# In the last tile of each sample, the first gate and value product is issued ahead of the next sample's projection

## The reference

```
x = x + tanh(g_xattn) * LN(rs * (softmax(clip(q k^T / sqrt(32))) v @ Wo^T + bo)) * gamma + beta   # q from LN(x), k and v from 64 context tokens, 16 heads
x = x + tanh(g_ffn) * bit_linear(silu(bit_linear(LN(x), gate_w)) * bit_linear(LN(x), val_w), out_w)
bit_linear(x, w): each token of x is scaled by 127 / max|x| and rounded to integers, w is rounded to -1, 0, 1 times its mean |w|
```

## Time and profile before

| | |
|---|---|
| time, median of 3 runs | 772.79 us (772.76 to 773.64) |
| the profiled execution's own time | 772.76 us |
| its span in the profile | 771.0 us |
| busy: TensorE, VectorE, ScalarE, GpSimd | 92%, 81%, 69%, 41% of the span |
| one pass of the loop body | about 80.2 us |

### The profile page before, as it was taken

One profiled execution on the slowest core, in us unless ns is written; L12 is line 12 of the kernel. 1 busy time (PEld: TensorE's weight loads), 2 busy tenths in 40 slices (PEclk: granted clock), 3 DMA queues, 4 the chain that ended last, 5 costly groups with the idle time before them and its releaser, 6 DMA issues.

```text
span 771.0 us, 13495 instructions
## 1 busy us (share of the span) xinstructions
PE 706.6 (92%) x4204; PEld 341.1 (44%) x4253; DVE 622.7 (81%) x1290; ACT 535.4 (69%) x701; POOL 316.9 (41%) x482
## 2 busy tenths in 40 slices
PE   4989755878999999999999999999999999999997
PEld 3434434433544454445444444444444544454443
DVE  6868797697778987798779877987798778778885
ACT  4575778977657956786678856795588657856554
POOL 4310315223554356344643454346444553354440
PEclk9999886989999999999999999999999999999999
DMA  9864426121453354435443354326433542244312
GB/s 324 254 232 124 116 83 212 42 39 45 113 130 67 83 111 105 106 82 109 95 116 82 80 124 90 85 63 129 106 79 81 115 96 62 55 93 86 83 42 69
DMA packets 177386, 81.07 MB, mean 105 GB/s; under 512 B 156595, under 2 KB 156851, under 8 KB 176710
## 3 DMA queue, kind: packets, MB, share of 16 engines
q1 hardware_dynamic: 177350, 80.62, 42.7%
HBM read 38.75 MB, written 10.51 MB: 64 GB/s over the span
## 4 chain that ended last, share of the span: by engine, by line
PE 37%; DVE 33%; issue 10%; ACT 6%; DMA 5%; another core or an unknown queue 5%; POOL 2%; SPq 1%; DVEq 0%; POOLq 0%; ACTq 0%
PE psum L1739 12%; PE psum L1705 11%; PE psum L1730 5%; DVE psum L1227 3%; DVE hmax L1240 2%; DMA arena<-x_both 2%; PE psum L1709 2%; DVE arena L1235 2%; PE psum L1932 2%; ACT arena L921 2%; DVE xmax L1312 2%; DVE stats L1300 2%; DVE arena L1346 2%; DVE stats L1266 2%
## 5 line engine op out<-in xcount | busy, mean ns | idle before, releaser
L1705 PE MATMUL psum<-ternary,xqT 128*128 128x512 f16 x1024 | 259.6, 382 | 3.2 <-DVE xqT L1257 1.1
L1705 PEld LDWEIGHTS psum<-ternary,xqT 128*128 128x128 f16 x1024 | 98.3, 98 | 120.3 <-DVE arena L1232 2.8
L665 POOL TENSOR_TENSOR rstd<-var_e,minus_half 128x1 f32<-128x1 f32 x64 | 39.8, 623 | 211.1 <-DVE var_e L1304 111.1
L1730 PE MATMUL psum<-ternary,arena 128*128 128x512 f16 x496 | 121.7, 379 | 1.5 <-DMA arena<-arena 1.5
L855 ACT ACTIVATE arena<-psum,dequant 128x512 f32<-128x512 f32 x128 | 87.1, 681 | 49.7 <-PE psum L1709 47.4
L1739 PE MATMUL psum<-wo_hi,arena 128*128 128x512 f16 x256 | 82.6, 384 | 0.3
L1240 DVE TENSOR_REDUCE hmax<-arena 128x1 f32<-128x1024 f32 x64 | 77.6, 1213 | 0.8
L1739 PE MATMUL psum<-arena,wq_hi 128*128 128x512 f16 x256 | 76.1, 379 | 1.7 <-DMA arena<-x_both 1.1
L863 ACT ACTIVATE arena<-arena,round_c,hscale 128x1024 f32<-128x1024 f32 x62 | 73.5, 1235 | 1.9 <-DVE hscale L1252 1.9
L895 ACT ACTIVATE arena<-arena,round_c 128x1024 f16<-128x1024 f32 x62 | 70.8, 1142 | 0.3
L1730 PEld LDWEIGHTS psum<-ternary,arena 128*128 128x128 f16 x496 | 46.2, 98 | 54.8 <-issue 3.8
(11 more groups left out here) (213 smaller groups left out, 1302.1 us busy)
## 6 DMA issues: line engine op xcount, KB each, us to landing
arena<-in_x SPq DMA_DIRECT2D x64, 256.0 KB, 2.8
out<-arena SPq DMA_DIRECT2D x31, 256.0 KB, 2.4
arena<-in_L_ffn_gate_w SPq DMA_DIRECT2D x4, 1024.0 KB, 12.9
arena<-in_L_ffn_out_w SPq DMA_DIRECT2D x3, 1024.0 KB, 4.9
ternary<-in_L_ffn_val_w SPq DMA_DIRECT2D x2, 1024.0 KB, 11.9
kcur<-k_scratch SPq DMA_DIRECT2D x56, 32.0 KB, 2.2
arena<-arena SPq DMA_TRANSPOSE x90, 3.1
ternary<-in_ctx SPq DMA_DIRECT2D x1, 1024.0 KB, 5.4
```

The source lines that it names most:

```text
L1705: ins = M.matmul(ps[:], xqT[:, t % 2, k, :], w[:, k, cols], start=(k == 0), stop=(k == KC - 1 and not biased))
L1730: ins = M.matmul(psO[:], hidT[t % 2][:, k, :], wo2[:, k, :], start=(k == 0), stop=(k == FC - 1))
```

## The change

In tile 3 of every sample, TensorE issues `gate_val(3, 0)` ahead of `project` (before: behind it). VectorE does `hidden(3, 0)` ahead of `statistics` (before: behind it), and `new_x` and `x_shift` behind `hidden(3, 1)` (before: behind `hidden(3, 0)`). No instruction is added or removed; ScalarE, GpSimd and the DMA queues keep their order. For b = 7 the attention part is off, so `project`, `statistics` and `new_x` are not there in tile 3 and the order stays as it was.

```diff
# VectorE, body
                     down = prev if t == 0 else ffn
+                    if ffn and t == NT - 1:
+                        hidden(t, 0)
                     if out_w_now and t == 0:
                         x_stats(c, t)
                     else:
                         statistics(update, pre, *nxt, t)
                     for n in range(NCH):
...
-                        if ffn:
+                        if ffn and (t < NT - 1 or n):
                             hidden(t, n)
...
-                        if n == 0:
+                        if n == (1 if ffn and t == NT - 1 else 0):
                             if update:
                                 new_x(*nxt)
                             if pre:
                                 x_shift(c, t)
# TensorE, body
                     attend = att and t == 2
+                    if ffn and t == NT - 1:
+                        gate_val(t, 0)
                     if update:
...
                             project(*nxt)
                     for i in range(NCH):
-                        if ffn:
+                        if ffn and (t < NT - 1 or i):
                             gate_val(t, i)
```

## The result

The changed kernel takes 779.26 us (median of 4 runs, 777.58 to 779.94) against 773.21 for the kernel before on the same chip: a ratio of 1.0081 [1.0053, 1.0107], 6.05 us slower. Forecast were 3.5. The profiled execution took 779.99 us, its span is 778.2 (before: 772.76 and 771.0).

What follows compares the result with a forecast made beforehand. TensorE and the chain over VectorE, GpSimd and the DMA transpose were taken to bound the kernel nearly together. The sum was 6 x 0.54 + 0.3 = 3.5 us on 772.76, giving 776.3 us, range 774.0 to 778.3.

Steps and rivals of the forecast that it cites:

- What bounds the kernel: At each boundary between passes, TensorE and the chain to query(0) arrive nearly together, the chain 0.17 us later.
- rival 1: TensorE is the bound and the early product fills its gaps: 2.0 us given back, 770.8 us; chance 0.07.
- Rivals 2 and 3: VectorE-GpSimd port: free, `new_x` takes 0.74 us, 774.3 us, chance 0.10; or lost, L708 precedes `new_x`, 783.4 us, chance 0.05.
- +1.94 and -1.40: Tile 3: `project` ends 1.94 us later; VectorE has one `hidden` (1.40 us) less between `project` and `x1_stats`.
- The steady pass: Query(0) to query(0): `x1_stats` and the transpose chain behind it come 0.54 us later per boundary; pass at 80.7 us.
- the input of `gate_val(3, 0)`: ScalarE's copy ends 0.18 us ahead of the slot, so no wait; up to 0.2 us per tile kept for the range.
- Seen twice on TensorE but paid once: TensorE stands some 0.3 us at the transpose of inv_cols, parallel to the chain, so the 0.54 us counts once.
- 0.3 to 0.7 us: Sign at the boundary: query(0)'s wait for the tile 3 transpose, instead of 0.17 us.
- The 0.17 us of the earlier trace: TensorE's wait for the transpose before query(0) at 550.05; the most TensorE gives back of what the chain gains.
- The last body: Boundary of b = 6: `quant` 0.54 us later, less 0.22 us idle before silu(0, 1), delays codes and `down`: +0.3 us.
- six equal boundaries: Boundaries b = 0 to 5, each costing 0.54 us, with a DMA transpose of 3.05 us on the chain.
- 0.3 for SyncE's queue: Range allowance: `result`, `h_low(c, 2)`, its transpose and the store move by 1.94 us; costed at 0, bounds 0 and 0.3.

Runs made afterwards that it cites:

- the swap: In tile 3, GpSimd does `h_low(c, 3)` ahead of `update_resid`: on the changed kernel 774.66 us (1.0018), on the kernel before 770.82 us (0.9974).
- the shorter statistics: Tile 3's first `bn_stats` over 64 of 512 columns, added to the swap: new order 772.24 us (0.9987), old order 769.76 us (0.9954).

## Why the prediction was wrong

**What bounds the kernel: right.** The chain over VectorE, GpSimd and the transpose decides together with TensorE. The change filled VectorE's gap at no cost to TensorE but 0.07 us, and still lost; rival 1 is out. Rivals 2 and 3 are out too: `new_x` took 1.06 us (before 1.07) and not 0.74, and GpSimd's L708 did not go first. By the rule on the port pair that the Trainium skill gives ("SBUF — State Buffer", "Who interferes with whom") the price stays while the phase does; the trace agrees with 1.06.

**+1.94 and -1.40: right.** From `gate_val(3, 0)`'s start to `x1_stats` 10.48 us were measured (545.69 - 535.21), 10.46 were forecast; VectorE's last idle time ahead of `statistics` was 0.46 where "less than 0.4" was said, a small miss that costs nothing.

**The steady pass: 0.54 forecast, 0.64 measured.** The terms: 0.54; the input of `gate_val(3, 0)`, costed at nothing, 0.07 (the slot came at 533.41 + 8 x 0.216 = 535.14, it started at 535.21); 0.02 in the interval; 0.01 from `x1_stats` to query(0) (10.31 for 10.30). Six boundaries: 3.8 us for 3.2.

**"Seen twice on TensorE but paid once": half right.** The forecast put TensorE's stall at 0.3 us and saw slack left behind it. Paid once it is: query(0) waits 0.19 us, no more than before, so both paths became later by the same amount. But TensorE's own path lost 0.69 us between the transposes and `project` (550.89 - 549.68 = 1.21, where before it was 544.96 - 544.44 = 0.52), and the swap shows that it alone costs the 0.6: 0.51 between the transposes of the codes and that of inv_cols (0.57 for 0.06, of which the row shows 0.35 as waiting), and 0.18 from there to `project` (0.47 for 0.29). The slack that I had between the paths wasn't there. Query(0) waiting "0.3 to 0.7 us" was wrong for that reason.

The 0.17 us of the earlier trace rows was misread too. It counts from the modelled end of the matmul ahead, which is shown 0.16 us longer than it holds back the next one. In the kernel before, the last matmul of this row

```profile
548.86 1.03 PE L1705 MATMUL psum<-ternary,xqT 128*128 128x512 f16 x4
```

started near 548.86 + 3 x 0.216 = 549.51, and query(0) at 550.05: 0.54 us for 0.216, so 0.33 us were to be had. The swap on GpSimd gave just that, where the prediction had put the limit at 0.17.

**The last body: 0.3 forecast, 0.63 measured.** I took the slack of silu(0, 1) on ScalarE (0.22 us). The first codes' transpose has no such slack. SyncE's queue and ScalarE, before and after:

```profile
708.92 0.69 ACT L855 ACTIVATE arena<-psum,dequant 128x512 f32<-128x512 f32 x1
...
710.75 3.42 SPq L486 DMA_TRANSPOSE arena<-arena  x2
```

```profile
716.17 0.67 ACT L855 ACTIVATE arena<-psum,dequant 128x512 f32<-128x512 f32 x1
...
717.98 3.38 SPq L486 DMA_TRANSPOSE arena<-arena  x2
```

silu(0, 0) stands directly behind `quant`. From the first of the two transposes' issues to `down` it is 5.43 us before (716.18 - 710.75) and 5.41 after (723.39 - 717.98), and that issue moved with the whole delay of `quant`.

**The first boundary: the step that failed.** The forecast summed six equal boundaries (6 x 0.54), with the transpose's 3.05 us taken from one of them and nothing put on its changing, in the sum or in the range. At the first one it took 4.3 to 4.7 us, because an instruction transfer fell into it: 1.2 to 1.3 us in the profile of after, and with TensorE's lower clock behind it another 1.7 in the other two profiles. In the kernel before, that boundary showed a wait of 0.33 us, twice that of the earlier trace rows; I read one boundary and multiplied.

**The sum.** 6 x 0.64 + 0.6 = 4.4; with 1.2 to 1.3 for the slow transpose 5.7, and up to 1.7 more in executions in which the clock fell. The runs gave 6.05 and 5.6. Without the first boundary's surprise the order costs 3.8 + 0.6 = 4.4 us, or 777.2, inside the range; with it the time lies 1 us above its top, 778.3. That the rest would have fallen inside is in part luck: the 0.33 us of the last body fit only because the range had room for two things that came out smaller, 0.2 us per pass at `gate_val(3, 0)` (0.07) and 0.3 for SyncE's queue.

## What to carry to other kernels

Where two paths arrive nearly together, price the delay on each of them to the end, with the time that an engine needs to get going again behind a wait, before calling one of them covered: taking away the later one (here 0.34 us by a swap on GpSimd) leaves the other's whole price. In this kernel the gain lay at what stands ahead of the last wait on the critical chain, not at the busiest engine: two GpSimd steps exchanged gave 0.26%, moving nine matmuls cost 0.8%. And when a sum multiplies one boundary, look at all of them, the first above all, and list what else runs on the queues near a transfer that the path waits for: here the other transfer moved by 2.5 us when the order of the instructions changed.

## What the runs showed of the hardware

- L494's DMA transpose of 3.0 us took 4.25 to 4.85 us in all eleven cases from the first boundary on in which an instruction transfer of 0.02 MB (q8) started 1.2 to 2.0 us behind its issue, in either order. At the same two places, with that transfer 2.55 us or more behind the issue, it took 3.02 to 3.15. One such transpose in the setup, issued near 92 us and 2.1 us behind another, took 4.3 to 5.05 in every profile, with a transfer 0.6 to 2.7 us behind it. The cause inside the queues stays open.
- Behind a wait of 2.06 and 2.12 us TensorE's granted clock was 0.59 and 0.60 over the next 4.2 us, with matmuls at the 1.2 GHz rate, and the pass took some 1.7 us more. Behind one of 1.65 us it stayed at 1.00 (2.4 GHz), in one profile. In the thirteen profiles these two are the only falls of the clock between 180 us and the end.
- From the transpose of inv_cols to the `project` of the next body it is 0.27 to 0.33 us in the kernel before (both profiles) at the four boundaries at which the loop goes back to its head, and 0.06 at the other three. In the changed kernel it is 0.47 to 0.50 at the four, and 0.20 to 0.22 at two others (0.06 at the last, which has no wait). So 0.2 to 0.3 us go with the way back to the loop's head in both orders; the 0.24 of "issue" shown in the new one are not the new order's own price, some 0.15 to 0.2 us here. In the old order with both the swap and the shorter statistics it was 0.06 at all seven, so that this time can be hidden. By what, no run isolates.
